# Two-block attention tail: an earlier divide on VectorE, a later normalisation on ScalarE, and another order on TensorE

## The reference

```
x = x + tanh(g_xattn[0]) * L0_xattn(layernorm(x), ctx)      # one head, softmax over 120 keys
x = x + tanh(g_ffn[0])   * L0_ffn(layernorm(x))             # top-2 of 12 experts
x = x + tanh(g_xattn[1]) * L1_xattn(layernorm(x), ctx)      # 16 heads of 16, then Wo and bo
x = x + tanh(g_ffn[1])   * L1_ffn(layernorm(x))             # fp8 linear, one scale for the whole tensor
```

## Time and profile before

| | |
|---|---|
| median of 3 runs | 393.37 us (392.44 to 394.28) |
| the profiled execution | 393.37 us, its span 391.6 us |
| PE busy | 347.3 us (89%) |
| DVE busy | 266.0 us (68%) |
| ACT busy | 230.8 us (59%) |
| POOL busy | 159.2 us (41%) |
| mean granted clock of PE | 0.947 |

### The profile page before, as it was taken

The page is one execution under the profiler, slowest core; times in us unless marked ns, Lnnn a source line. Parts: engine busy times, 40 slices in busy tenths (PEclk is TensorE's granted clock), DMA queues, the critical chain, the costliest instruction groups (busy, mean ns, idle before and its releaser), DMA issues.

```text
span 391.6 us, 9083 instructions
## 1 busy us (share of the span) xinstructions
PE 347.3 (89%) x2955; PEld 268.6 (69%) x2956; DVE 266.0 (68%) x677; ACT 230.8 (59%) x462; POOL 159.2 (41%) x215
## 2 busy tenths in 40 slices
PE   1979999966899999999999998879999999989174
PEld 1768878644688888888888884556666666756142
DVE  1637887894645665555454456878889988685896
ACT  2387799530455555555555542466778678747685
POOL 6386589703255555555556524421132033001000
PEclk9969999975899999999999999999999999999776
DMA  7998381311132343423322304310011000000014
GB/s 191 329 419 332 145 365 57 110 28 40 40 95 94 108 133 103 123 68 80 80 73 67 87 30 145 112 56 22 35 56 55 2 2 2 3 2 2 0 42 175
DMA packets 15387, 38.26 MB, mean 98 GB/s; under 512 B 3574, under 2 KB 4748, under 8 KB 13820
## 3 DMA queue, kind: packets, MB, share of 16 engines
q1 hardware_dynamic: 9978, 22.55, 16.2%
q0 software_dynamic: 3936, 10.45, 9.2%
q10 hardware_dynamic: 1442, 4.85, 3.2%
HBM read 24.34 MB, written 13.50 MB: 97 GB/s over the span
## 4 chain that ended last, share of the span: by engine, by line
PE 71%; DVE 9%; ACT 8%; DMA 5%; issue 4%; ACTq 1%; SPq 1%; POOL 0%; DVEq 0%
PE two L1738 14%; PE two L1872 5%; PE two L1726 5%; PE two L1727 5%; PE two L1728 5%; PE two L1757 4%; PE two L1937 4%; PE two L1902 4%; PE two L1858 3%; PE two L1838 3%; DMA wl<-in_wmoe 3%; PE two L1748 2%; PE two L1929 2%; PE two L1595 1%; ACT wh L667 1%
## 5 line engine op out<-in xcount | busy, mean ns | idle before, releaser
L539 POOL DMA_INDIRECT xg<-xn_d,slot_i x39 | 37.8, 968 | 65.3 <-PE two L1748 51.1
L1222 DVE SCALAR_TENSOR_TENSOR gate<-th,two 128x512 f32<-128x512 f32 x39 | 26.8, 687 | 42.8 <-ACT th L738 42.8
L1726 PE MATMUL two<-wh,gh 128*128 x156 | 47.3, 303 | 0.2
L545 POOL DMA_INDIRECT y_d<-y_sb,goal_i x39 | 38.5, 988 | 20.5 <-ACT y_sb L748 10.5
L738 ACT ACTIVATE th<-two 128x512 f32<-128x512 f32 x39 | 23.3, 597 | 35.5 <-PE two L1738 35.5
L1727 PE MATMUL two<-wl,gh 128*128 x156 | 44.0, 282 | 0.0
L1728 PE MATMUL two<-wh,gl 128*128 x156 | 43.9, 282 | 0.0
L1757 PE MATMUL two<-ident,gate 128*128 128x128 f32 x156 | 41.9, 272 | 0.0
L559 POOL TENSOR_TENSOR rstd<-var,half 128x2 f32<-128x2 f32 x14 | 9.8, 701 | 76.7 <-DVE var L1289 76.7
L1322 DVE TENSOR_REDUCE nm<-two 128x8 f32<-128x960 f32 x32 | 36.1, 1151 | 4.5 <-PE two L1858 4.1
L512 POOL TENSOR_TENSOR wl<-wl,wh 128x512 fp32r<-128x512 f32 x28 | 35.2, 1275 | 9.8 <-ACT wh L667 9.8
(11 more groups left out here) (267 smaller groups left out, 892.0 us busy)
## 6 DMA issues: line engine op xcount, KB each, us to landing
wl<-in_wmoe SPq DMA_DIRECT2D x8, 1024.0 KB, 14.5
y_d<-wh ACTq DMA_DIRECT2D x4, 1024.0 KB
yg<-y_d SPq DMA_DIRECT2D x7, 512.0 KB, 3.6
xn_d<-xq SPq DMA_DIRECT2D x8, 256.0 KB, 2.0
xz<-xn_d SPq DMA_DIRECT2D x8, 256.0 KB, 2.6
out_x<-of SPq DMA_DIRECT2D x8, 256.0 KB, 2.0
x_sb<-in_x SPq DMA_DIRECT2D x1, 1024.0 KB, 7.9
x_sb<-in_x SPq DMA_DIRECT2D x1, 768.0 KB, 4.5
```

The lines of the kernel that those rows point to most:

```text
L539: pool.indirect_dma_start(xg[:, n % 2, :], None, xn_d, bass.IndirectOffsetOnAxis(ap=slot_i[:, n:n + 1], axis=0)).then_inc(gathered[n % 2], 16)
L545: pool.indirect_dma_start(y_d, bass.IndirectOffsetOnAxis(ap=goal_i[:, n:n + 1], axis=0), y_sb[:, n % 2, :], None).then_inc(y_stored[n % 2] ...
L1222: dve.scalar_tensor_tensor(gate[:, k, :], th[:], 1.0, bank[2 + k][:], ALU.add, ALU.mult).then_inc(gate_ok, 1)
L1726: pe.matmul(dst, gh[:, k, a], wh[:, bass.ds(w, D)], start=c == 0, stop=False)
```

## The change

ACT: in the last turn of the loop (`t == B + 1`) `norm3(4)` stood ahead of `copy_oT(6)`; it now stands behind it, as in all other turns.

DVE: in the turn `t == B`, `divide(6, 1)` stood between `maxima(7, 1, 0)` and `maxima(7, 1, 1)`; it now stands ahead of both.

PE, behind `transpose_o(6, 1)`: the order was the bias, `transpose_max(7)`, both halves of `project(6, 0)`, `less_maxima(7, 0)`, the first half of `project(6, 1)`. It is now the bias, both halves of `project(6, 0)`, `transpose_max(7)`, the first half of `project(6, 1)`, `less_maxima(7, 0)`. What follows is the same.

```diff
@@ ACT
-                if t == B + 1:
-                    norm3(t - 5)
                 if 0 <= t - 3:
                     copy_oT(t - 3)
-                if 0 <= t - 5 and t < B + 1:
+                if 0 <= t - 5:
                     norm3(t - 5)
@@ DVE
                 divide(t - 2, 0)
+                if t == B:
+                    divide(t - 2, 1)
                 maxima(t - 1, 1, 0)
-                divide(t - 2, 1)
+                if t < B:
+                    divide(t - 2, 1)
                 maxima(t - 1, 1, 1)
@@ PE
             transpose_o(B - 2, 1)
-            pe.wait_ge(oT_ok, B - 1)
-            start_projection(B - 2)
+            project(B - 2, 0)
             transpose_max(B - 1)
-            for c in range(C):
-                project_half(B - 2, 0, c, False)
+            project_half(B - 2, 1, 0, False)
             less_maxima(B - 1, 0)
-            project_half(B - 2, 1, 0, False)
             scores_by_key(B - 1, 1, FIRST)
```

## The result

Over 20 runs of each kernel the changed one has a median of 397.61 us (393.00 to 402.58), the kernel before 392.60 us (390.61 to 394.28): +5.0 us, +1.3%. The ratio, 1.0088 with a 95% interval from 1.0061 to 1.0114, leaves out executions more than 1.5% above the fastest of their kernel; here these are part of what the change does, so the spread is shown too. The forecast was 394.6, the range ended at 395.9. The forecast was built on 393.37, which is 0.8 us above the median of 20 runs, so the +5.0 stands against a forecast of +1.25.

What follows compares the result with a forecast made beforehand. PE was taken to bound the kernel, with 71% of the chain. DVE 1.20, ACT 0 and PE order 0.05 gave 1.25 us, so 393.37 + 1.25 = 394.6 us, range 393.0 to 395.9.

Steps and rivals of the forecast that it cites:

- The DVE term: The divide ahead of the last scores' maxima: DVE must wait for its transposes, so maxima and scores_by_key(7,0) start later, +1.20 us.
- The ACT term: norm3(4) behind copy_oT(6): largest_of(4) starts 1.4 us later but slack remains, cost 0; up to 1.08 us without cover.
- The PE order term: Both halves of project(6, 0) ahead of transpose_max(7): less_maxima and its copy meet within 0.01 us; +0.05 us, bounds 0 and 0.4.
- The rival on ACT: The exponentials fit by only 0.04 us; if less_maxima comes 0.4 us late, ACT becomes the bound: 395.3 us, chance 0.08.
- The clock falls in the new hole: PE idles 2.0 instead of 0.8 us ahead of scores_by_key(7,0), its clock falls: 2.5 us more, 397.1, chance 0.05.
- The clock of the last stage: Rival: the later start shifts the clock's change there, faster bias and linear products give back 1.3 us: 393.3, chance 0.10.

Runs made afterwards that it cites:

- e1: The kernel before with only the DVE part of the change, divide(6,1) ahead of both maxima: median 395.35 us, ratio 1.0051.
- e5: The changed kernel with one product that nothing reads in PE's hole ahead of scores_by_key(7,0): median 395.17 us, ratio 1.0092.
- e7: The changed kernel as it is, run again beside the others on one chip: median 399.65 us over six runs, ratio 1.0181.
- e9: The changed kernel with one unread product where PE waits for the copy of oT, the long hole kept: median 394.17 us, ratio 1.0054.
- e3: The changed kernel with three products that nothing reads in PE's hole ahead of scores_by_key(7,0): 393.29 us, ratio 1.0025.
- e2: The kernel before with only the PE and ACT parts of the change, DVE as before: 392.29 us, ratio 0.9995.
- e8: The kernel before with the PE and ACT parts, plus ten unread products in PE's two idle stretches ahead of the last stage: 391.45 us, ratio 0.9965.
- e4: The kernel before with four products that nothing reads in PE's hole ahead of scores_by_key(7,0): 393.31 us, ratio 1.0015.
- e6: The changed kernel with two unread reductions of x on DVE ahead of the maxima, widening PE's hole: median 397.04 us, ratio 1.0126.

## Why the prediction was wrong, point by point

**The DVE term was right.** The wait was put at +1.20 us; A grew from 4.48 to 5.67, by 1.19, in the change, e1, e5, e7 and e9 alike, and to 5.68 in e3. The divide started 0.69 us after its transposes and PE's hole was 1.96 us, both as worked out.

**The ACT term was right.** `norm3(4)` runs behind the copy at 348.90, and `largest_of(4)` waited 0.62 us on DVE, ahead of a longer idle time; B in e2 shows no loss.

**The PE order term was mis-sized and had the wrong sign.** It was +0.05 and measured -0.23 us (B, 9.97 against 10.20). Rows of e2's timeline of PE, and behind them the row of the kernel before that stands in the last one's place:

```profile
347.58 0.50 PE L1931 MATMUL two<-bo,one 2*128 2x512 f32 x1 [0.69 <-ACT oT L846]
...
349.83 0.50 PE L1870 MATMUL two<-nmT,sel 32*120 32x256 f32 x8
350.16 0.40 PE L1870 MATMUL two<-qh,know 32*120 32x256 f32 x4
...
351.20 0.70 PE L1935 MATMUL two<-wo_sb,oT 128*128 128x256 f32 x2
...
354.26 0.70 PE L1937 MATMUL two<-wo_sb,oT 128*128 128x256 f32 x2
```

Up to `less_maxima` the sum held: it was put 2.27 us behind the bias and came 349.83 - 347.58 = 2.25 behind it. What was off lies behind it. `less_maxima` now stands directly ahead of the keys of the next group, of the same 32-row shape, and the two take 351.20 - 349.83 = 1.37 us to the start of the next half; apart, with a half of the projection between, they took 0.44 us (352.07 to 352.51) and 1.13 us (353.13 to 354.26), 1.57 together. The sum took the durations over from the old neighbours. Together, 1.19 - 0.23 = 0.96 us is what the edits cost at full clock; e3, where the clock doesn't fall, is 0.7 us above the kernel before by the medians.

**The rival on ACT didn't come.** The four exponentials run without a gap, 3.77 us from 353.37 in the change, and B shows no loss by it in e2.

**The step that failed: the sum has no term for TensorE's clock.** "The clock falls in the new hole" was dismissed with a chance of 0.05 and priced at nothing in 1.20 + 0 + 0.05, and it is what happened: B lies 1.51 us above its value at full clock in the first profile of the change and 6.05 us in the second. The argument against it was that PE idled 3.98 us before 366.32 and the stretch to 366.4 still read 1.00. That row was read as if the clock answered at once. In the changed kernel too the clock reads 1.00 through the hole and for two microseconds behind it, and falls at 349.3; in the kernel before the fall showed in the very next row, 0.60 from 366.4 on the earlier trace rows. The row told of a clock that can answer late, not of a hole that is harmless. The second idle time, 0.69 us ahead of the bias, wasn't counted at all, and e9 suggests that it had a part.

**The rival's price.** It was 2.5 us on top of the forecast, 397.1 in all; the median came out at 397.6. That the two are so near is luck: the base was 0.8 us high, and there is no one price. A low stretch of 3.4 us cost 1.51 us in the profiles of the change, e1 and e5 alike, one of 13.7 us cost 6.05 us in e7, and the median, at the lower edge of the upper group, hangs on how many runs fall in each. The difference of the two prices, 4.5 us, is about that of the groups' medians, 4.7. Which of the two an execution gets, no run here explains.

**The clock of the last stage gave nothing back.** Its four bias products took 2.04 us in the change as in the kernel before, and from the last projection to the end it was 31.2 against 31.0 us. The rival's price was low, too: at full clock in e8 they took 1.16 us, 0.9 less, where the earlier trace rows had been read as 0.5.

**What the skill says beside it.** That gaps in PE's work throttle its clock and that what follows starts cold (the Trainium skill, "TensorE: Matmul & The Clock Gate", section "HAM oscillation — how this bites in real kernels") agrees with the change's windows, 0.50 from 349.4 to 352.4. The waits in the page's own case are longer, about 3 to 5 us; that 1.53 to 1.97 us of idling, with 0.69 us soon after, is enough, only the runs here show. The same page says of another kernel that frequent micro-idles make the clock fall and rise as well (section "A second HAM failure mode: psum-queue depth-cycling"); e9 fits it, with 1.96 us of idling kept, 0.44 us of the second removed, and no fall up to 362 us in its one profile.

**Shown and not shown.** Shown: the divide alone brings it (e1), the order doesn't (e2), delay without idling doesn't (e4), and shortening PE's hole with the delay kept cures it (e3). Open: why one execution stays at 1.2 GHz for 3.4 us and another for 13.7, and how much of the fall is due to the second idle time (e9).

## What to carry to other kernels

A wait that is added to TensorE costs its own length and, on top, may cost the clock of all that follows; price both, and count all idle times near each other, not only the new one. A window that still reads 1.00 just behind an idle time proves nothing: look at the rows that follow it, here up to 3 us further. Where TensorE must wait on another engine, a few products that nothing reads, into a free PSUM place, can be worth more than the order of the rest, and where times fall in two groups, look at the granted clock of each run before comparing medians.

## What the runs showed of the hardware

- The clock fell 2.2 (e7), 2.5 (the change, e1) and 3.0 us (e5) after the end of a hole of 1.53 to 1.97 us, and inside the hole when that was 3.15 us (e6). With holes of 0.77 (before) and 0.67 us (e3), and the same 0.69 us behind them, it didn't fall there.
- At 1.2 GHz PE was busy without a break from 352.0 to 363.6 us in e7, and the clock was still 0.50; it came back after 13.7 us in all, in the first profile of the same program after 3.4 us, in e6 after 10.2.
- The values of the last batch took 3.57 us at 1.2 GHz and 1.91 at 2.4; the four 256-column products of the projection 2.00 (the change) and 1.06 (e2).
- Matmuls of one shape behind each other were quicker than the same ones with another shape between: 1.37 (e2) against 0.44 + 1.13 us (before).
